# Probabilities copied in two parts, and the normalisations moved to ScalarE, in an attention kernel with a planned order

## The chip, the cores and the metric

The kernel runs on one core of one Trainium2 chip. The metric is the device time of one execution in microseconds (us). The core has five instruction streams: PE (TensorE, matrix products), DVE (VectorE), ACT (ScalarE), POOL (GpSimd) and SP (SyncE), which here only issues DMAs. Each stream works off its list in order; between streams, semaphores hold an instruction back until the other engine has passed a count. 16 DMA engines move data. A tile lies over 128 partitions; matrix products arrive in PSUM, which the kernel uses as 8 banks of 512 float32 columns.

## The reference

Input is x of shape (8, 512, 128): 8 batches, 512 positions, 128 features. With xn = layernorm(x) it computes

```
out = x + attention(xn) + ffn(xn)

attention:  q, k, v = xn @ W_qkv, 16 heads of 64; rotary embedding on q and k
            p = softmax(causal(q k^T / 8));   (p v) @ W_out
ffn:        q, k, v = xn @ Wq + bq, ...;      16 heads of 8, full softmax, no mask
            x2 = xn + layernorm(ctx @ Wo + bo)*g1 + be1
            gate = softmax(x2 @ Wg + bg); the two best of 8 experts, weighted
            x2 + layernorm(moe)*g2 + be2
```

All in float32. Three layer normalisations per batch: of x (called xn), of the inner attention's output (nm1) and of the experts' sum (nm2).

## The kernel before

The 8 batches are worked off one behind the other, each with T = 4 tiles of 128 positions. The causal attention of a batch goes in NC = 8 chunks c of two heads. For one chunk the steps are: `proj` (PE) makes q and k; `raw` (ACT) brings them to SBUF; `swap` (SP, L1134) exchanges neighbouring rows by two DMAs, for the rotary embedding; `rope`, `hi`, `lo` (POOL, L1196 to L1211) rotate and split them into two parts of reduced precision; `sc` (PE, L1694) makes the scores, in three units: unit 0 is query tile 3 with 512 keys, unit 1 is tiles 2 and 0 with 384 and 128, unit 2 is tile 1 with 256; `max` (DVE, L1580), `exp` (ACT, L1338); `tr` (DVE, L1588) transposes blocks of 32x32 of the probabilities in place, one step per unit; `shuf` (SP, L1140) copies them from `pn` to `pt` by four DMAs, one for each quarter of 32 source partitions, which completes the transposition; `pv` (PE, L1708) multiplies them with v; `div` (DVE, L1599) scales the result.

A tile of probabilities for 128 queries and 128 keys is "one tile" in `pn`; a chunk has 10 of them for each head (1 + 2 + 3 + 4). In `pn` and `pt` the 10 tiles of a head stand side by side, so a DMA moves runs of 2 heads x 10 tiles x 32 columns x 4 bytes = 2560 bytes, 128 runs in each. `pn` has two buffers, `pt` one: `shuf` also waits until `pv` of the chunk before is done.

The inner attention's steps (`fsm`, `fmax` L1458, `fmT`, `fst`, `fexp` L1293, `fpv` L1758 and others) stand between those of the chunks. The normalisations are done so: `ln`, `ln1`, `ln2` (DVE) make mean and variance and write `spread`; `rs0`, `rs1`, `rs2` (POOL, L1188) raise it to the power -0.5; `xn`, `nm1`, `nm2` (DVE, L1384) subtract the mean and multiply, in four instructions on 128x128. `x2` and `out` (POOL, L1218) work on with nm1 and nm2.

The order of each stream is written out by numbers: `PLACE` has a place for every step, and `ORDER` sorts the steps of an engine by it. `PSUM` has the bank of every product. `after(step)` is the semaphore and the count at which the step is done; `wait` leaves out what the stream has already waited for.

Of the kernel before, what the change touches and what calls it, by code (L numbers as in the profile page):

```python
# [9 lines left out]
ALU = mybir.AluOpType  # L10
ACT = mybir.ActivationFunctionType
# [3 lines left out]
P = 128  # L15
# [27 lines left out]
TILES_OF = {3: 0, 2: 4, 0: 7, 1: 8}  # L43
UNIT_TILES = [slice(0, 4), slice(4, 8), slice(8, 10)]
PT_N = T * (T + 1) // 2
# [13 lines left out]
        [78],  # L59
        [197],  # L60
        [326],
        [456],
        [585],
        [716],
        [842],
    ],
    "tt": [
        [5],
    ],
    "proj": [  # L70
# [8 lines left out]
    ],  # L79
    "tb": [  # L80
        [2],
    ],
    "fqk": [
        [1],
        [86],
        [213],
        [342],
        [472],
        [601],
        [729],  # L90
        [858],
    ],
    "fv": [
        [8],
        [121],
        [249],
        [378],
        [509],
        [636],
        [764],  # L100
        [897],
    ],
    "fsm": [
# [8 lines left out]
    ],  # L112
    "fmT": [
        [14, 30, 58, 83],
        [131, 153, 189, 212],
        [260, 282, 318, 343],
        [388, 411, 446, 471],
        [517, 540, 576, 600],
        [646, 668, 704, 730],
        [775, 798, 830, 857],  # L120
        [903, 926, 963, 985],
    ],
    "fst": [
# [8 lines left out]
    ],  # L132
    "fpv": [
# [8 lines left out]
    ],  # L142
    "sc": [
        [23, 26, 28, 35, 46, 47, 52, 53, 56, 73, 74, 75, 88, 93, 95, 101, 102, 104, 116, 119, 120, 124, 127, 129],
        [147, 148, 150, 161, 178, 179, 181, 182, 183, 203, 204, 205, 219, 220, 221, 228, 229, 237, 244, 247, 250, 254, 257,
         258],
        [276, 277, 279, 290, 307, 308, 310, 312, 314, 332, 333, 334, 348, 350, 351, 357, 358, 363, 375, 377, 379, 383, 384,
         387],
        [405, 406, 409, 419, 435, 437, 438, 441, 443, 461, 462, 463, 476, 480, 482, 485, 486, 492, 504, 505, 507, 512, 513,
         515],  # L150
        [534, 535, 536, 548, 564, 565, 567, 568, 571, 590, 591, 594, 605, 609, 611, 615, 616, 619, 633, 634, 637, 639, 644,
         645],
        [663, 664, 667, 677, 692, 693, 696, 697, 699, 719, 720, 721, 735, 736, 739, 744, 745, 753, 762, 765, 766, 770, 772,
         773],
        [792, 793, 796, 806, 822, 823, 825, 827, 831, 848, 849, 850, 862, 866, 868, 873, 874, 881, 891, 892, 895, 901, 902,
         904],
        [921, 922, 923, 935, 951, 952, 955, 957, 958, 976, 977, 978, 991, 993, 996, 1000, 1001, 1004, 1013, 1015, 1016, 1020,
# [3 lines left out]
        [31, 33, 38, 45],  # L161
        [154, 156, 160, 170],
        [283, 285, 289, 300],
        [412, 414, 418, 429],
        [542, 543, 547, 557],
        [670, 672, 676, 686],
        [799, 801, 805, 816],
        [928, 929, 934, 945],
    ],
# [9 lines left out]
    ],  # L179
    "fT": [  # L180
        [48, 71, 91, 114],
        [177, 199, 226, 243],
        [303, 330, 356, 373],
        [439, 457, 478, 499],
        [561, 587, 607, 631],
        [690, 714, 743, 758],
# [1663 lines left out]
```

## Time and profile before

| | us |
|---|---|
| median of three runs | 1407.32 |
| the three runs | 1400.66, 1407.32, 1414.51 |
| the profiled execution | 1420.66 |
| its span, first to last instruction | 1418.8 |

| engine | busy us | share of the span |
|---|---|---|
| PE | 1110.0 | 78% |
| DVE | 1034.0 | 73% |
| POOL | 857.6 | 60% |
| ACT | 742.4 | 52% |

The mean granted clock of TensorE is 0.861 of its full 2.4 GHz. The 16 DMA engines are busy 40% of the span by SP's queue and move 139 MB at 98 GB/s, 320 KB in each of the 256 DMAs of the probabilities. A share of busy time is a mean over stages; what stands in the way in one place is to be read from the chain of waits and the waits by engine.

### The profile page before, as it was taken

The numbers are of one execution on the slowest core, as the hardware profiler recorded it, in microseconds if no ns is written. First come the engines' busy times: TensorE is split into PE (matmuls) and PEld (weight loads), VectorE is DVE, ScalarE is ACT, GpSimd is POOL, SyncE is SP. The second block draws the span as 40 slices with busy tenths as digits, with TensorE's granted clock in tenths as the row PEclk, the third lists the DMA queues.
The fourth block names the chain that finished last, engine by engine and source line by source line (L and its number), as shares of the span: only waits on it lengthen the run. The fifth ranks groups of instructions, "written<-read, shape, count | busy, mean of one in ns | idle before, by whom it ended". The sixth has DMA issues, their size and how long they took to land.

```text
span 1418.8 us, 23791 instructions
## 1 busy us (share of the span) xinstructions
PE 1110.0 (78%) x8474; PEld 662.9 (47%) x8474; DVE 1034.0 (73%) x2404; ACT 742.4 (52%) x1665; POOL 857.6 (60%) x728
## 2 busy tenths in 40 slices
PE   4778789687886878887798777877889678897866
PEld 2334446344452444544464444544546335463534
DVE  6966679767786767965788657777768766787646
ACT  3656455564544645555455644547545464555731
POOL 3658766657665485576564756656676555744940
PEclk8799979899798978988889886998969888698978
DMA  5163632455224442434524363244542245425342
GB/s 158 41 135 86 147 88 60 108 127 119 64 73 110 116 121 60 96 87 116 123 64 108 83 147 77 68 104 112 124 108 71 72 96 119 112 64 123 81 93 66
DMA packets 77793, 139.27 MB, mean 98 GB/s; under 512 B 11494, under 2 KB 23016, under 8 KB 77676
## 3 DMA queue, kind: packets, MB, share of 16 engines
q1 hardware_dynamic: 74204, 134.80, 39.8%
q10 hardware_dynamic: 3472, 2.95, 0.7%
q8 instruction: 68, 1.11, 0.3%
q14 instruction: 49, 0.40, 0.1%
HBM read 5.60 MB, written 2.10 MB: 5 GB/s over the span
## 4 chain that ended last, share of the span: by engine, by line
PE 36%; DVE 20%; DMA 17%; SPq 12%; POOL 7%; issue 4%; ACT 3%; ACTq 1%; POOLq 0%; DVEq 0%
DMA pt<-pn 12%; PE work L1708 10%; SPq L1140 10%; DVE fnmax L1458 7%; PE work L1758 4%; PE work L1694 4%; DVE pn L1588 4%; DMA swapped<-raw 4%; PE work L1616 3%; PE work L1724 3%; PE work L1618 3%; PE work L1617 3%; PE work L1733 3%; DVE work L1540 2%; DVE branch L1543 2%
## 5 line engine op out<-in xcount | busy, mean ns | idle before, releaser
L1196 POOL TENSOR_TENSOR raw<-raw,cos_t 128x512 f32<-128x512 f32 x128 | 163.5, 1277 | 406.4 <-DMA swapped<-raw 390.5
L1293 ACT ACTIVATE fpt<-work 128x1024 f32<-128x1024 f32 x256 | 251.9, 1026 | 202.0 <-PE work L1748 192.7
L1458 DVE TENSOR_REDUCE fnmax<-work 128x2 f32<-128x1024 f32 x256 | 302.4, 1215 | 59.1 <-PE work L1733 58.0
L1338 ACT ACTIVATE pn<-work,nmax 128x512 f32<-128x512 f32 (+3 forms) x512 | 266.0, 537 | 140.5 <-DVE nmax L1580 139.8
L1708 PE MATMUL work<-pt,v 128*32 128x384 f32 (+2 forms) x2560 | 211.9, 493 | 118.0 <-DMA pt<-pn 113.1
L1580 DVE CUSTOM_DVE_ANT_0 work<-work,causal 128x512 f32<-128x512 f32 (+3 forms) x512 | 236.6, 515 | 81.2 <-PE work L1694 80.8
L1708 PEld LDWEIGHTS work<-pt,v 128*32 128x32 f32 x2560 | 100.2, 136 | 228.4 <-issue 154.7
L1588 DVE STREAM_TRANSPOSE pn<-pn 128x1024 f32<-128x1024 f32 (+1 forms) x192 | 198.6, 1048 | 3.3 <-ACT pn L1338 3.2
L1211 POOL TENSOR_TENSOR qk_l<-raw,qk_h 128x512 fp32r<-128x512 f32 x128 | 180.0, 1413 | 3.4
L1200 POOL TENSOR_TENSOR raw<-raw,swapped 128x512 f32<-128x512 f32 x128 | 164.3, 1284 | 10.0
L1197 POOL TENSOR_TENSOR swapped<-swapped,sin_t 128x512 f32<-128x512 f32 x128 | 164.6, 1286 | 0.0
L1599 DVE TENSOR_TENSOR u<-work,l_wide 128x512 f32<-128x512 f32 x64 | 43.8, 685 | 149.5 <-PE work L1708 140.7
L1318 ACT COPY raw<-work 128x512 f32<-128x512 f32 x128 | 75.3, 588 | 127.3 <-PE work L1618 84.9
L1758 PE MATMUL work<-fpt,fv 128*9 128x512 f32 x1024 | 140.5, 646 | 1.3 <-ACT pn L1338 1.3
L1694 PE MATMUL work<-qk_h 64*128 64x512 f32 (+3 forms) x512 | 105.2, 403 | 46.5 <-POOL qk_l L1211 23.3
L1733 PE MATMUL work<-fqs 32*128 32x512 f32 x512 | 73.8, 565 | 62.4 <-DVE fnmax L1458 18.4
L1206 POOL CAST qk_h<-raw 128x512 fp32r<-128x512 f32 x128 | 108.4, 859 | 14.6 <-PE work L1694 12.8
L1338 ACT ACTIVATION_READ_ACCUMULATOR pn<-work,nmax 128x1 f32 x512 | 108.5, 212 | 0.0
L1694 PEld LDWEIGHTS work<-qk_h 64*128 64x128 f32 x512 | 53.8, 201 | 105.0 <-issue 47.5
L1748 PE MATMUL work<-fqm,fqs 32*128 32x512 f32 x512 | 71.9, 549 | 32.2 <-DVE fnmax L1458 5.9
L1694 PE MATMUL work<-qk_l,qk_h 64*128 64x512 f32 (+3 forms) x512 | 90.5, 344 | 0.0
L1694 PE MATMUL work<-qk_h,qk_l 64*128 64x512 f32 (+3 forms) x512 | 90.2, 344 | 0.0
(153 smaller groups left out, 1893.0 us busy)
## 6 DMA issues: line engine op xcount, KB each, us to landing
pt<-pn SPq DMA_DIRECT2D x256, 320.0 KB, 5.7
swapped<-raw SPq DMA_DIRECT2D x256, 128.0 KB, 2.3
fqs<-fqn SPq DMA_DIRECT2D x96, 128.0 KB, 2.7
x_in<-in_L_attn_x_dram SPq DMA_DIRECT2D x8, 256.0 KB, 4.7
out_dram<-x_in SPq DMA_DIRECT2D x7, 256.0 KB, 2.3
fpt<-in_L_attn_W_qkv_dram ACTq DMA_DIRECT2D x3, 512.0 KB, 6.2
pn<-in_L_ffn_We_dram ACTq DMA_DIRECT2D x1, 512.0 KB, 9.7
wout<-in_L_attn_W_out_dram ACTq DMA_DIRECT2D x1, 512.0 KB, 12.5
```

Source lines behind the costliest of these rows:

```text
L1196: nc.gpsimd.tensor_tensor(raw[:, n % 3], raw[:, n % 3], cos_t[:], ALU.mult)
L1197: nc.gpsimd.tensor_tensor(swapped[:, n % 2], swapped[:, n % 2], sin_t[:], ALU.mult).then_inc(pool_link, 1)
L1200: nc.gpsimd.tensor_tensor(raw[:, n % 3], raw[:, n % 3], swapped[:, n % 2], ALU.add).then_inc(done["rope"], 1)
L1211: nc.gpsimd.tensor_tensor(turned(qk_l[:, c % 2, k], k), plain(raw[:, n % 3], k), turned(qk_h[:, c % 2, k].bitcast(F32), k), ALU.subtract). ...
L1293: nc.scalar.activation(fpt[:, ((b * G + g) * T + i) % FP, 2 * r:2 * r + 2].rearrange("p h n -> p (h n)"), bank_of(("fst", b, g, i), 2 * r, 2),
L1338: ins = nc.scalar.activation(pn[:, c % 2, :, h, tiles].rearrange("p c i r -> p i c r"), bank_of(("sc", b, c, unit), h)[:, at:at + n].rearr ...
L1458: nc.vector.tensor_reduce(fnmax[:, j, 2 * r:2 * r + 2, 0:1], bank_of(("fsm", b, g, j), 2 * r, 2).rearrange("p (f n) -> p f n", f=2), AX.X, ...
L1580: ins = nc.vector.tensor_tensor_reduce(out=scores, in0=scores, in1=causal[:, S - n:S], scale=-1.0 / math.sqrt(DH), scalar=3.0e38, op0=ALU.add,
L1588: nc.vector.transpose(blocks, blocks).then_inc(done["tr"], 1)
L1694: ins = nc.tensor.matmul(bank_of(x_, h)[:, at:at + (j + 1) * P], left[rows, c % 2, 0, tile(j)], right[rows, c % 2, 1, 0:(j + 1) * P], star ...
L1708: ins = nc.tensor.matmul(psum[a:a + STRIP, at:at + len(js) * P], v[:, i, 2 * c + h, a % DH:a % DH + STRIP], moving.rearrange("p a j r -> p ...
L1758: ins = nc.tensor.matmul(psum[f * STRIP:f * STRIP + FVW], fv[:, i, g * GH + f], fpt[:, ((b * G + g) * T + i) % FP, f], start=i == 0, stop= ...
```

## The change

1. `pn` and `pt` become two tiles each. Part 0 has the 8 tiles of units 0 and 1 (query tiles 3, 2 and 0), part 1 the 2 tiles of unit 2 (query tile 1). The step `shuf` copies part 0 in four DMAs with runs of 2048 bytes, 256 KB each, and waits for the transpose of unit 1; a new step `shu2` copies part 1 in four DMAs with runs of 512 bytes, 64 KB each, and waits for the transpose of unit 2. Both wait for `pv` of the chunk before; `pv` and the next use of `pn` wait for both. The four quarters are now issued in the order 0, 2, 1, 3.
2. `pv` has seven groups of four matmuls instead of five, since a product with three query tiles at once (384 columns) would reach over both parts; the number of columns is the same.
3. `xn`, `nm1`, `nm2` go from DVE to ACT, as an activation with scale and bias from columns: x * rstd + shift. DVE makes -mean in one more small instruction (L1413), POOL multiplies it with rstd in one more (L1201). DVE loses 96 instructions and gains 24, ACT gains 96, POOL gains 24.
4. Small single-column tiles are put together, and some loads at the start go to other places of SBUF, so that the tiles fit.
5. `PLACE` and `PSUM` are new throughout.

SP's list in the second batch, before, around the copies of its first three chunks (L1134 the swaps, L1140 the copies, L1147 copies for the inner attention):

```order
L1134 DMA swapped<-raw 64x512 x2
L1140 DMA pt<-pn 128x1x640 x4
L1134 DMA swapped<-raw 64x512 x6
L1140 DMA pt<-pn 128x1x640 x4
L1134 DMA swapped<-raw 64x512 x2
L1147 DMA fqs<-fqn 32x2x512
L1147 DMA fqs<-fqn 32x1024
L1147 DMA fqs<-fqn 32x2x512
L1134 DMA swapped<-raw 64x512 x2
L1140 DMA pt<-pn 128x1x640 x4
```

and the same three chunks after the change (L1144 the swaps, L1150 both copies: 128x1x512 is the large part, 128x1x128 the small one):

```order
L1150 DMA pt<-pn 128x1x128 x4
L1144 DMA swapped<-raw 64x512 x2
L1150 DMA pt<-pn 128x1x512 x4
L1144 DMA swapped<-raw 64x512 x4
L1150 DMA pt<-pn 128x1x512 x4
L1144 DMA swapped<-raw 64x512 x2
L1150 DMA pt<-pn 128x1x128 x4
L1157 DMA fqs<-fqn 32x2x512
L1157 DMA fqs<-fqn 32x1024
L1157 DMA fqs<-fqn 32x2x512
L1150 DMA pt<-pn 128x1x128 x4
L1144 DMA swapped<-raw 64x512 x2
```

The large copy of the third chunk follows as the next row. In the first and the third chunk the small part is issued ahead of the large one, in the second behind it. Over the whole program the small part stands first in 24 of 64 chunks.

DVE's list after the change, from the transpose of unit 1 of the second of these chunks to that of unit 2 (ISA rows are the masked maxima and the reads of their results):

```order
L1605 STREAM_TRANSPOSE pn<-pn 128x8x128
L1596 ISA work,nmax<-work,causal 128x256
L1596 ISA nmax 128x1
L1596 ISA work,nmax<-work,causal 128x512
L1596 ISA nmax 128x1
L1596 ISA work,nmax<-work,causal 128x512
L1596 ISA nmax 128x1
L1610 RECIPROCAL l_inv<-l_sum 128x8
L1596 ISA work,nmax<-work,causal 128x384
L1596 ISA nmax 128x1
L1596 ISA work,nmax<-work,causal 128x128
L1596 ISA nmax 128x1
```

The transpose of unit 2 is the next row. In the list before, two maxima and one `div` stood between the two transposes of this chunk; how much stands between them differs from chunk to chunk in both lists.

The diff, without the tables of numbers:

```diff
-TILES_OF = {3: 0, 2: 4, 0: 7, 1: 8}
-UNIT_TILES = [slice(0, 4), slice(4, 8), slice(8, 10)]
-PT_N = T * (T + 1) // 2
+PT_N = [2 * T, T // 2]
+PT_OF = {3: (0, 0), 2: (0, T), 0: (0, 2 * T - 1), 1: (1, 0)}
+UNIT_AT = [(0, slice(0, T)), (0, slice(T, 2 * T)), (1, slice(0, T // 2))]
...
     "xT": [
         [0],
-        [78],
-        [197],
+        [75],
+        [201],
...
-        pn = sb("pn", [P, 2, QUADS, 2, PT_N, STRIP])
-        pt = sb("pt", [P, QUADS, 2, PT_N, STRIP])
+        pn = [sb(f"pn{n}", [P, 2, QUADS, 2, tiles, STRIP]) for n, tiles in enumerate(PT_N)]
+        pt = [sb(f"pt{n}", [P, QUADS, 2, tiles, STRIP]) for n, tiles in enumerate(PT_N)]
...
-                elif kind == "shuf":
-                    c = x_[2]
-                    wait(sp, after("tr", b, c, 2))
+                elif kind in ("shuf", "shu2"):
+                    c, part = x_[2], int(kind == "shu2")
+                    wait(sp, after("tr", b, c, 1 + part))
                     wait(sp, after("pv", *ring(1, b, c, NC)))
-                    for a in range(QUADS):
-                        sp.dma_start(pt[:, a].rearrange("p h n r -> p (h n r)"),
-                                     pn[a * STRIP:(a + 1) * STRIP, c % 2].rearrange("p c h n r -> p c (h n r)")).then_inc(shuf_done[c % 2], 16)
+                    for a in (0, 2, 1, 3):
+                        sp.dma_start(pt[part][:, a].rearrange("p h n r -> p (h n r)"),
+                                     pn[part][a * STRIP:(a + 1) * STRIP, c % 2].rearrange("p c h n r -> p c (h n r)"))                            .then_inc((shuf_done, shu2_done)[part][c % 2], 16)
...
-                    nc.gpsimd.tensor_tensor(rstd[:, n], spread[:, n], power[:], ALU.pow).then_inc(done[kind], 1)
+                    nc.gpsimd.tensor_tensor(rstd[:, n], spread[:, n], power[:], ALU.pow).then_inc(pool_link, 1)
+                    links += 1
+                    pool.wait_ge(pool_link, links)
+                    nc.gpsimd.tensor_tensor(shift[:, n], shift[:, n], rstd[:, n], ALU.mult).then_inc(done[kind], 1)
...
+            def normalise(kind, n, dst, src):
+                for t in range(T):
+                    ins = nc.scalar.activation(dst(t), src(t), ACT.Identity, scale=rstd[:, n, t:t + 1], bias=shift[:, n, t:t + 1])
+                ins.then_inc(done[kind], 1)
...
+                elif kind == "xn":
+                    wait(act, after("rs0", b))
+                    wait(act, after("x2T", b - 2))
+                    wait(act, after("res", b - 2))
+                    normalise("xn", 0, lambda t: xn[:, b % 2, t], lambda t: x_in[:, b % XB, t])
...
+                nc.vector.tensor_scalar(shift[:, n].unsqueeze(2), moments[:, n, :, 0:1], -1.0, None, ALU.mult)
                 nc.vector.tensor_scalar(spread[:, n].unsqueeze(2), moments[:, n, :, 1:2], EPS, None, ALU.add)\
                     .then_inc(done[kind], 1)
-
-            def normalise(kind, n, dst, src):
-                for t in range(T):
-                    ins = nc.vector.tensor_scalar(dst(t), src(t), moments[:, n, t, 0:1], rstd[:, n, t:t + 1],
-                                                  ALU.subtract, ALU.mult)
-                ins.then_inc(done[kind], 1)
...
                     wait(pe, landed("shuf", b, c))
+                    wait(pe, landed("shu2", b, c))
                     if c == 0:
                         wait(pe, after("vc", b, T - 1))
-                    for i, js in ((0, (3, 2, 1)), (0, (0,)), (1, (3, 2, 1)), (2, (3, 2)), (3, (3,))):
-                        first, at = TILES_OF[js[0]] + i, (T - 1 - js[0]) * P
+                    for i, js in ((0, (3, 2)), (0, (0,)), (0, (1,)), (1, (3, 2)), (1, (1,)), (2, (3, 2)), (3, (3,))):
+                        part, first = PT_OF[js[0]]
+                        first, at = first + i, (T - 1 - js[0]) * P
```

## Rows read from the trace of the kernel before

**Rows 1.** The page, part 1: busy us of each engine (share), instructions.

```profile
PE 1110.0 (78%) x8474; PEld 662.9 (47%) x8474; DVE 1034.0 (73%) x2404; ACT 742.4 (52%) x1665; POOL 857.6 (60%) x728
```

**Rows 2.** The page, part 4: the chain that ended last, by engine and line.

```profile
PE 36%; DVE 20%; DMA 17%; SPq 12%; POOL 7%; issue 4%; ACT 3%; ACTq 1%; POOLq 0%; DVEq 0%
DMA pt<-pn 12%; PE work L1708 10%; SPq L1140 10%; DVE fnmax L1458 7%; PE work L1758 4%; PE work L1694 4%; DVE pn L1588 4%; DMA swapped<-raw 4%; PE work L1616 3%; PE work L1724 3%; PE work L1618 3%; PE work L1617 3%; PE work L1733 3%; DVE work L1540 2%; DVE branch L1543 2%
```

**Rows 3.** Chain in order of time, one chunk: start us, us, what.

```profile
889.55 0.59 SPq L1140
...
890.83 1.98 SPq L1140
...
892.85 5.98 DMA pt<-pn
...
898.97 2.37 PE work L1708 x40
```

**Rows 4.** Chain in order of time, the PV step of another chunk.

```profile
775.16 4.50 PE work L1708 x40
```

**Rows 5.** Windows, both PV steps: us, PE, PEld, DVE, ACT, POOL busy; PEclk, DMA, GB/s.

```profile
775.10:779.70 4.60, 4.54 (x44) 2.16 (x44) 0.00 (x0) 0.00 (x0) 0.01 (x1) 0.50 0.33 101
898.90:901.40 2.50, 2.43 (x42) 1.48 (x44) 0.48 (x1) 1.00 (x5) 2.42 (x3) 1.00 0.57 180
```

**Rows 6.** Chain in order of time, a swap behind a copy.

```profile
104.97 4.16 DMA swapped<-raw
```

**Rows 7.** Waits: of PV before L1708; of POOL: us, times, longest.

```profile
  DMA pt<-pn: 147.2, 50
...
POOL raw L1196 <- DMA swapped<-raw: 390.5, 75, 15.3
```

**Rows 8.** The page, part 6: DMA issues, KB each, median us to landing.

```profile
swapped<-raw SPq DMA_DIRECT2D x256, 128.0 KB, 2.3
...
out_dram<-x_in SPq DMA_DIRECT2D x2, 128.0 KB, 1.8
```

**Rows 9.** Timeline of SP's queue at the start: start us, us, line.

```profile
10.97 0.43 SPq L1124 DMA_DIRECT2D affine<-in_L_ffn_be_dram  x1
```

**Rows 10.** Windows as in rows 5, through one copy with nothing beside it.

```profile
196.00:197.25 1.25, 1.25 (x9) 1.25 (x7) 1.25 (x2) 0.59 (x1) 0.00 (x0) 0.50 0.91 104
197.25:198.50 1.25, 1.25 (x8) 1.25 (x7) 0.13 (x1) 0.00 (x0) 0.00 (x0) 0.50 1.02 221
198.50:199.75 1.25, 1.25 (x8) 0.93 (x7) 0.39 (x2) 0.00 (x0) 0.00 (x0) 0.50 0.88 131
199.75:201.00 1.25, 1.25 (x12) 0.13 (x8) 1.05 (x9) 0.89 (x1) 0.04 (x1) 0.50 0.87 268
```

**Rows 11.** Groups by form, DVE: busy us, mean ns, idle before.

```profile
L1384 DVE TENSOR_SCALAR branch<-branch,moments,rstd 128x128 f32<-128x128 f32 x32 | 20.1, 699 | 1.7 <-POOL rstd L1188 1.7
...
L1384 DVE TENSOR_SCALAR xn<-x_in,moments,rstd 128x128 f32<-128x128 f32 x32 | 14.9, 532 | 0.0
...
L1384 DVE TENSOR_SCALAR branch<-work,moments,rstd 128x128 f32<-128x128 f32 x32 | 10.9, 402 | 7.7 <-POOL rstd L1188 7.7
...
L1379 DVE TENSOR_SCALAR spread<-moments 128x4 f32<-128x4 f32 x24 | 7.0, 291 | 0.8
```

**Rows 12.** Chain in order of time, the longest piece of L1384.

```profile
1122.36 4.93 DVE branch L1384 x4
```

**Rows 13.** Groups by form, PE, ACT, POOL: busy us, mean ns, idle before.

```profile
L1708 PE MATMUL work<-pt,v 128*32 128x384 f32 x1024 | 150.4, 664 | 118.0 <-DMA pt<-pn 113.1 <-ACT pn L1338 4.9
...
L1708 PE MATMUL work<-pt,v 128*32 128x128 f32 x1024 | 66.0, 331 | 0.0
...
L1708 PE MATMUL work<-pt,v 128*32 128x256 f32 x512 | 51.7, 475 | 0.0
...
L1338 ACT ACTIVATE pn<-work,nmax 128x128 f32<-128x128 f32 x128 | 48.3, 377 | 0.0
...
L1188 POOL TENSOR_TENSOR rstd<-spread,power 128x4 f32<-128x4 f32 x24 | 24.4, 1019 | 84.2 <-DVE spread L1379 84.2
```

More of the change, by code:

```diff
@@ L91 @@
-        [858],
+        [338],
+        [471],
+        [600],
+        [730],
+        [859],
     ],
     "fv": [
[L94 to L101, printed above, removed]
+        [6],
+        [115],
+        [242],
+        [377],
+        [505],
+        [633],
+        [760],
+        [890],
     ],
     "fsm": [
[8 rows of a table removed]
[8 rows of a table added]
     ],
     "fmT": [
-        [14, 30, 58, 83],
-        [131, 153, 189, 212],
-        [260, 282, 318, 343],
@@ L260 @@
     "smh": [
-        [2],
+        [5],
     ],
     "wh": [
-        [0, 1, 10],
+        [0, 2, 4],
+    ],
+    "xn": [
+        [1],
+        [52],
+        [169],
+        [309],
+        [437],
+        [557],
+        [688],
+        [823],
     ],
@@ L403 @@
-        [994],
+        [138],
+        [267],
+        [397],
+        [525],
+        [654],
+        [783],
+        [912],
+        [1015],
+    ],
+    "nm1": [
+        [145],
+        [274],
+        [403],
+        [533],
+        [661],
+        [790],
+        [922],
+        [1024],
     ],
     "x2h": [
-        [151],
-        [278],
-        [403],
-        [531],
-        [656],
-        [781],
-        [908],
-        [1005],
+        [155],
+        [284],
+        [413],
+        [542],
+        [671],
+        [800],
+        [929],
+        [1030],
@@ L414 @@
     ],
     "gexp": [
-        [156],
-        [283],
-        [409],
-        [535],
-        [661],
-        [787],
-        [913],
-        [1011],
+        [160],
+        [293],
+        [418],
+        [547],
+        [676],
+        [805],
+        [934],
+        [1034],
+    ],
+    "nm2": [
+        [198],
+        [338],
+        [468],
+        [579],
+        [715],
+        [856],
+        [968],
+        [1037],
     ],
@@ L427 @@
         [12],
-        [98],
-        [264],
-        [391],
-        [542],
-        [704],
-        [847],
+        [95],
+        [261],
+        [401],
+        [547],
+        [678],
+        [830],
     ],
     "turn": [
-        [8],
-    ],
-    "str": [
-        [4],
-    ],
-    "xn": [
-        [2],
-        [40],
-        [216],
-        [364],
-        [509],
-        [650],
-        [801],
-        [945],
-    ],
-    "strl": [
-        [5],
-    ],
-    "wl": [
-        [1, 7, 21],
-    ],
-    "xl": [
-        [6],
-        [91],
-        [227],
-        [375],
-        [526],
-        [669],
-        [812],
-        [959],
-    ],
-    "sml": [
-        [3],
-    ],
+        [4],
+    ],
+    "str": [
+        [2],
+    ],
+    "strl": [
+        [3],
+    ],
+    "wl": [
+        [1, 6, 7],
+    ],
+    "xl": [
+        [5],
+        [88],
+        [228],
+        [372],
+        [515],
+        [652],
+        [796],
+        [943],
+    ],
+    "sml": [
+        [8],
+    ],
     "qkb": [
-        [9],
+        [10],
     ],
@@ L608 @@
+        [298],
+        [441],
+        [583],
+        [727],
+        [869],
+        [1011],
+        [1121],
     ],
     "ln1": [
-        [163],
-        [308],
-        [455],
-        [601],
-        [746],
+        [159],
+        [303],
+        [446],
+        [590],
+        [733],
+        [876],
+        [1020],
+        [1126],
+    ],
+    "x2l": [
+        [173],
+        [316],
+        [459],
+        [602],
+        [745],
+        [888],
+        [1030],
+        [1140],
+    ],
@@ L615 @@
+    "gsub": [
+        [177],
+        [320],
+        [463],
+        [607],
+        [750],
         [893],
-        [1040],
-        [1149],
-    ],
-    "nm1": [
-        [166],
-        [312],
-        [458],
-        [604],
-        [750],
-        [896],
-        [1041],
+        [1035],
+        [1143],
+    ],
+    "pick": [
+        [179],
+        [327],
+        [464],
+        [608],
+        [751],
+        [894],
+        [1036],
+        [1145],
+    ],
+    "moew": [
+        [186, 190, 191, 192],
+        [329, 333, 334, 335],
+        [472, 476, 477, 478],
+        [615, 619, 620, 621],
+        [758, 762, 763, 764],
+        [901, 905, 906, 907],
+        [1043, 1047, 1048, 1049],
+        [1147, 1148, 1149, 1151],
+    ],
@@ L979, in build @@
         power = sb("power", [P, T])
-        spare = sb("spare", [P, 1])
-        value_bias = sb("value_bias", [P, 1])
-        warm = sb("warm", [P, 1])
+        singles = sb("singles", [P, 3])
+        spare, value_bias, warm = (singles[:, n:n + 1] for n in range(3))
         x_in = sb("x_in", [P, XB, T, D])
@@ L1015, in build @@
         spread = sb("spread", [P, 3, T])
+        shift = sb("shift", [P, 3, T])
         rstd = sb("rstd", [P, 3, T])
-        gmax = sb("gmax", [P, T])
-        gsum = sb("gsum", [P, T])
-        grec = sb("grec", [P, T])
+        gate_cols = sb("gate_cols", [P, 3, T])
+        gmax, gsum, grec = (gate_cols[:, n] for n in range(3))
         gexp = sb("gexp", [P, T, E])
@@ L1043, in build @@
         shuf_done = [sem(f"shuf{n}_done") for n in range(2)]
+        shu2_done = [sem(f"shu2{n}_done") for n in range(2)]
         x_loaded = [sem(f"x{n}_loaded") for n in range(XB)]
@@ L1288, in _ @@
                     if b == 0:
+                        wait(act, after("tt", 0))
                         for n in range(3):
@@ L1484, in _ @@
                     statistics("ln1", 1, lambda t: src[:, t])
-                elif kind == "nm1":
-                    src = bank_of(("wo", b)).rearrange("p (t d) -> p t d", d=D)
-                    wait(dve, after("rs1", b))
-                    wait(dve, after("out", b - 1))
-                    normalise("nm1", 1, lambda t: branch[:, t], lambda t: src[:, t])
                 elif kind == "gsub":
```

600 lines of the change are left out of this document (268 added, 332 removed), and 441 rows, old and new, of tables (PLACE, PSUM).

## The prediction

> **What bounds the kernel now.** I read the page's busy shares first [rows 1]: the busiest engine, PE, works 78% of the span. No engine is full, so the time lies in waits between engines that each take their work in a fixed order. The chain that ended last says which waits [rows 2]: PE 36%, DVE 20%, DMA 17%, SP's queue 12%. By line, the copy pt<-pn (12%), its issues (L1140, 10%) and the PV matmuls behind it (L1708, 10%) are a third of the chain. One chunk in order of time shows the link [rows 3]: SP starts its four issues right behind the last transpose, at 889.55; the third takes 1.98 us where the first takes 0.59; the last byte lands at 898.83, 9.3 us after the first issue; then PV runs. The waits agree [rows 7]: PE and its weight loader stand 147 us for this copy, 50 times, 2.9 us each.
>
> Two things hang on that copy. After such a wait PE is slow: the same 40 PV instructions take 2.37 us in one chunk [rows 3] and 4.50 us in another [rows 4], with a granted clock of 1.00 and 0.50 [rows 5], that is 2.4 and 1.2 GHz; before the slow ones PE had stood idle for the copy. And the swap DMAs of the rotary embedding wait in SP's queue behind the copy: at 104.97 the chain goes through one that needs 4.16 us to land [rows 6], where 2.3 is the median [rows 8]. Swaps are 4% of the chain, some 50 us, so 12 pieces of this size; pt<-pn, 12.4% of 1418.8 us at 6.0 us each, is 28 or 29 pieces. About 40 of 64 chunks have their copy on the chain in one way or the other.
>
> **The change, term by term**, in us against the profiled execution's own 1420.66 (span 1418.8).
>
> *A, early start of the large part.* The copy of the tiles of units 0 and 1 no longer waits for the last transpose. What this gives depends on the new order. In it 24 of the 64 chunks have the small copy ahead of the large one in SP's queue, as the first and third chunk shown there; there SP waits for the last transpose before anything moves, and nothing starts early. In 18 of the other 40 the two transposes stand next to each other on DVE (under 1 us of work between). In 22 there is DVE work between, 1.2 to 11 us by the durations of its rows; the piece shown for DVE is some 3.6 us. Where it is long, the path from the last transpose shrinks from 9.3 us to four issues at about 0.6 and a landing like that of 128 KB in 512-byte runs, 1.8 us [rows 8]: 4.4 us, so at most 4.9 is gained. Cut off at that, the 22 gain 3.2 on average, 70 us together; 24 of these fall to chunks 0 and 7 of a batch, which have 10 us and more of other PE work before PV. The other 46, at a chance of about a half of being on the chain: **-22**. Bounds 0 and -45.
>
> *B, swaps behind the copy.* Eight issues stand before a swap instead of four. Four issues of 128 runs cost 0.43 us each when the queue is free [rows 9], 0.6 in the copy itself: 1.7 to 2.4 us later, less what the large ones gain by moving 256 KB instead of 320. 12 pieces at +0.8: **+10**. Bounds 0 and 12 x 2.4 = +29.
>
> *C, chunks without a gap.* The same bytes in eight DMAs. The large ones start 0.6 us earlier, the added issues and completions eat that. 42 chunks, of which 18 on the chain, at +0.3: **+5**. Bounds -0.6 and +1.2 each: -11 and +22.
>
> *D, order of the four quarters (0, 2, 1, 3).* The diff also changes this. In a copy with nothing beside it the rate falls to 131 GB/s in one stretch of 1.25 us and is 268 in the next [rows 10]; with 130 + 276 KB before it, the slow stretch lies in the second quarter of 328 KB and the fast one mostly in the third. If the slow one ran like the fast one, a set would save 0.64 us, 40 sets 26. I take half: **-13**. Bounds +12 (the mixture disturbs, 0.3 a set) and -52 (twice the gain). The Trainium skill (SBUF — State Buffer, section Door 1: The DMA port swizzle) says that partitions 0 to 63 reach only the 8 even DMA ports and 64 to 127 the odd ones, which would make quarters 0 and 1 rivals and 0 and 2 not. The same section also says that the ports are picked by one transfer's span and two transfers can't be fused; by that this term would be nothing and the sum 13 higher.
>
> *E, DVE.* The normalisations go: 20.1 + 14.9 + 10.9 = 45.9 us; 24 copies of the mean are added at 0.29 us, 7.0 [rows 11]. Of the 39 us saved little is on the path: L1384 is under the 2% at which the chain's list ends, with one long piece of 4.93 us in which DVE went at a quarter of its pace beside POOL [rows 12]. **-7**, bounds 0 and -20 (all at DVE's share, 20 of 73%, is 11).
>
> *F, ScalarE.* 96 new instructions on 128x128. Nearest row: the exponential of the same shape, with one column operand, 377 ns [rows 13]; 36 us. ScalarE is 3% of the chain at 52% busy, so a sixteenth: **+2**, bounds 0 and +15 (normalisations held up in its queue). The Trainium skill (ScalarE: Activation LUTs, section What ACT_TABLE_LOAD costs) gives 186 ns + 0.833 ns per element and 93 ns for each column operand; with two that is an estimate of 479 ns, 46 us, and would change this term by less than one. The same page's rules for kernel authors send such adds and multiplies to VectorE; no row shows the rule deciding here, where ScalarE is the freer engine.
>
> *G, POOL.* 24 more tiny operations at 1.02 us [rows 13], 24 us, on the way to every normalised tile; POOL's share of the chain is a ninth of its busy time: **+3**, bounds 0 and +15.
>
> *H, PV.* Seven groups of four matmuls instead of five, the same columns. Busy per group: 384 columns 150.4/256 = 0.59 us, 256 columns 51.7/128 = 0.40, 128 columns 66.0/256 = 0.26 [rows 13]. Before 2 x 0.59 + 0.40 + 2 x 0.26 = 2.10; now 3 x 0.40 + 4 x 0.26 = 2.24. With 44 PV steps on the chain (10.4%, 148 us, so 3.4 us each), a part of them at half clock: **+8**, bounds +6 and +18.
>
> *I, clock.* PV is 1.0 us a chunk above its fast 2.37. If five of the shortened waits leave PE warm, at 2.1 each: **-10**, bounds +5 and -25.
>
> Sum: -22 + 10 + 5 - 13 - 7 + 2 + 3 + 8 - 10 = **-24 us**, 1.7%. The profiled execution is 13 us above the median of the three runs (1407.32); 1.7% of that is 24 as well, so **1384 us** is the forecast, 1397 for a profiled execution like this one. The order on PE I count at nothing: between one PV and the next it has the same kinds of steps in nearly the same places in both.
>
> **Rivals.**
>
> *R1, slower: SP's queue becomes the wait.* Third and fourth issues of a set take 1.9 us [rows 3], because the queue accepts no more until something ahead of it is done. If that is counted in DMAs or runs and not in bytes, the added four do not cost 0.6 but more. Place: the chunks without a gap and the swaps, 18 + 12 on the chain. It decides from about 0.8 us an issue on, where it has eaten the 24; at 1.0 us it is 4 x 0.4 x 30 = +48, so +24: **1431**. For it: the 1.98; and POOL already stands 390 us for swaps [rows 7]. Against it: small issues in a row at 0.43 [rows 9]. The Trainium skill (DMA: Bandwidth & Descriptors, section Bandwidth) tells to batch DMAs to 1 MiB and gives about 2.0 us + bytes/436e3 for each; paid one after the other for four more DMAs of 64 KB that would be an estimate of 8.6 us a chunk. The trace does not bear this out for a set: four of 320 KB would be 11 us by it, and land in 9.3.
>
> *R2, no change: the waits only move.* The new order uses the early start in 22 chunks alone; DVE's maxima and PE's own work take over as the chain (20 and 36% already), D is worth nothing. Then -24 + 13 + 11 = 0: **1407**.
>
> *R3, more: the copy itself gets faster.* If quarters from both halves run as the fast stretch does, -1.3 us a set, and the waits fall under what cools PE: D -52, I -20, the rest as it is: -24 - 39 - 10 = -73: **1335**. For it: the rate halves where nothing else moves. Against: the first stretch is slow too, and no order changes that.
>
> **How the numbers follow.** Forecast 0.38, R2 0.27, R3 0.18, R1 0.17. What can be told from no change is 1%, 14 us. Faster than 1393: R3, most of the forecast (0.32) and a little of R2 (0.04): 0.54. Within: 0.27. Slower than 1421: R1 and a little of R2: 0.19. The range from 1342 to 1424 cuts off about half of R3 and half of R1, one in ten on each side; the bounds of A and D, not added up, lie within it. The forecast's own range is 1365 to 1400.
>
> **What would show it.** A: first large issue ahead of the last transpose in about 22 chunks; PE's wait for pt down from 147 to 110 us or so; if it stays, A is wrong. B and R1: the issue durations of the 512-byte copies, 0.6 or near 1.9; POOL's wait for swaps beyond 390. D: first issue to last landing of the large part under 7.4 us (four fifths of 9.3). E, F: DVE busy near 995, ScalarE near 780. H: L1727 busier by about 9 us at the same clock. I: mean granted clock over 0.87. What would make it wrong above all is D, which no row measures, and an order that is worse on DVE in a way that counts of rows do not show.

## The result: 2% slower, and the profile after

| | before | after |
|---|---|---|
| median of four runs each, us | 1406.02 | 1434.65 |
| lowest and highest | 1400.66, 1414.51 | 1432.18, 1442.0 |
| the profiled execution, us | 1420.66 | 1432.18 |
| mean granted clock in it | 0.861 | 0.853 |

The ratio is 1.0207 with an interval of 1.0143 to 1.027: the change made the kernel slower by 29 us. The forecast was 1384 us, 24 us faster, with a range from 1342 to 1424.

Busy us of each engine after, as in [rows 1], and the chain that ended last, as in [rows 2]:

```profile
PE 1103.1 (77%) x9498; PEld 697.0 (49%) x9498; DVE 993.1 (69%) x2332; ACT 776.3 (54%) x1761; POOL 862.2 (60%) x752
...
PE 43%; DVE 20%; SPq 14%; DMA 8%; ACT 7%; issue 6%; POOL 3%; ACTq 0%; DVEq 0%; POOLq 0%
```

DVE lost 41 us of work and ScalarE gained 34, as foreseen. The chain has less DMA (8% for 17%) and more PE (43% for 36%). So the transfers hold up the end less. The waits of the engines (us in total, times, longest), and the one for the copy in the kernel before:

```profile
POOL raw L1209 <- DMA swapped<-raw: 377.6, 70, 16.8
DVE u L1616 <- PE work L1727: 207.2, 41, 9.1
PEld work L1727 <- issue: 198.7, 224, 8.2
...
PE work L1727 <- DMA pt<-pn: 140.3, 33, 8.0
```

```profile
PE work L1708 <- DMA pt<-pn: 113.1, 38, 5.3
```

PE's wait for the copy went from 113 us in 38 pieces to 140 in 33, and the longest from 5.3 us to 8.0: fewer waits, and longer ones. The issues (KB each, median us to landing), first before and then after, rule out that DMAs got slower:

```profile
pt<-pn SPq DMA_DIRECT2D x256, 320.0 KB, 5.7
...
pt<-pn SPq DMA_DIRECT2D x256, 256.0 KB, 4.4
swapped<-raw SPq DMA_DIRECT2D x256, 128.0 KB, 2.1
pt<-pn SPq DMA_DIRECT2D x256, 64.0 KB, 2.2
```

A swap took 2.3 us before [rows 8]. A long wait is then to be looked for ahead of the issue. In the third chunk of the third batch, SP's queue, then DVE, then PE (start us, us, engine, line):

```profile
436.91 6.46 SPq L1144 DMA_DIRECT2D swapped<-raw  x4
443.47 6.83 SPq L1150 DMA_DIRECT2D pt<-pn  x8
```

```profile
433.57 1.23 DVE L1605 STREAM_TRANSPOSE pn<-pn 128x1024 f32<-128x1024 f32 x1
...
439.74 0.70 DVE L1605 STREAM_TRANSPOSE pn<-pn 128x512 f32<-128x512 f32 x1
```

```profile
454.25 4.50 PE L1727 MATMUL work<-pt,v 128*32 128x256 f32 x56 [6.58 <-DMA pt<-pn]
```

The transpose of unit 1 ends at 434.80. From there on the large copy could go: the PV of the chunk before is done. But SP's list has four issues of swaps first; these wait for ScalarE's `raw`, the third of them until 442.3, and end at 443.4. Then comes the small copy, 3.5 us, and only then the large one, at 447.0: **12.2 us after its inputs were ready**, and 6.6 after the last transpose. PE stands for 6.58 us, and its clock is at half after that:

```profile
451.00:454.20 3.20, 0.00 (x0) 0.00 (x0) 0.00 (x0) 0.91 (x3) 1.59 (x2) 0.50 0.61 170
454.20:458.80 4.60, 4.55 (x60) 3.01 (x60) 0.00 (x0) 0.00 (x0) 0.00 (x0) 0.50 0.00 0
```

(Windows as in [rows 5]; the granted clock is the 0.50.) Over all 64 chunks, I took for each copy (after the change, for each large one) the moment at which its last transpose and the PV before it had ended, and its first issue. Before, the issues lay 27 us behind these moments in all. After, the large ones lay 247 us behind: by the step that stands directly ahead, 16 chunks behind a swap that itself waited (113 us), 16 behind their own small copy (112; in the chunk above the swaps stood ahead of that in turn), the rest behind copies for the inner attention and a load. By the position of the chunk in its batch, the third is the worst: its first large issue came 0.7 us after the last transpose before, and 8.8 after the change. That is the theory for the experiments.

### The profile page after: what moved, and what is told of

It reads as the page before. It is cut to its first block, busy times and chain, and to the rows that moved or that the text cites. A ratio compares the mean times of both kernels' runs of the same rounds, so it can differ in the third digit from the quotient of the medians.

```text
span 1430.3 us, 26155 instructions
## 1 busy us (share of the span) xinstructions
PE 1103.1 (77%) x9498; PEld 697.0 (49%) x9498; DVE 993.1 (69%) x2332; ACT 776.3 (54%) x1761; POOL 862.2 (60%) x752
## 3 DMA queue, kind: packets, MB, share of 16 engines
q8 instruction: 76, 1.25, 0.4%
## 4 chain that ended last, share of the span: by engine, by line
PE 43%; DVE 20%; SPq 14%; DMA 8%; ACT 7%; issue 6%; POOL 3%; ACTq 0%; DVEq 0%; POOLq 0%
PE work L1727 12%; SPq L1150 11%; DVE fnmax L1482 7%; DMA pt<-pn 6%; PE work L1633 5%; PE work L1635 4%; PE work L1634 4%; PE work L1711 4%; DVE pn L1605 3%; DVE work L1596 3%; PE work L1777 3%; PE work L1752 3%; ACT pn L1372 2%; ACT fpt L1313 2%; PE work L1767 2%
## 5 line engine op out<-in xcount | busy, mean ns | idle before, releaser
L1209 POOL TENSOR_TENSOR raw<-raw,cos_t 128x512 f32<-128x512 f32 x128 | 163.6, 1278 | 377.9 <-DMA swapped<-raw 377.6
L1727 PE MATMUL work<-pt,v 128*32 128x128 f32 (+1 forms) x3584 | 212.7, 406 | 168.3 <-DMA pt<-pn 140.3
L1727 PEld LDWEIGHTS work<-pt,v 128*32 128x32 f32 x3584 | 142.8, 139 | 240.8 <-issue 198.7
L1777 PE MATMUL work<-fpt,fv 128*9 128x512 f32 x1024 | 137.5, 635 | 0.7 <-ACT pn L1372 0.7
L1711 PE MATMUL work<-qk_h 64*128 64x512 f32 (+3 forms) x512 | 101.9, 391 | 24.0 <-POOL qk_l L1224 6.4
L1711 PEld LDWEIGHTS work<-qk_h 64*128 64x128 f32 x512 | 50.9, 193 | 80.4 <-issue 28.2
L1711 PE MATMUL work<-qk_l,qk_h 64*128 64x512 f32 (+3 forms) x512 | 86.4, 330 | 0.0
L1711 PE MATMUL work<-qk_h,qk_l 64*128 64x512 f32 (+3 forms) x512 | 86.3, 329 | 0.0
```

The source lines that it names most:

```text
L1209: nc.gpsimd.tensor_tensor(raw[:, n % 3], raw[:, n % 3], cos_t[:], ALU.mult)
L1711: ins = nc.tensor.matmul(bank_of(x_, h)[:, at:at + (j + 1) * P], left[rows, c % 2, 0, tile(j)], right[rows, c % 2, 1, 0:(j + 1) * P], star ...
L1727: ins = nc.tensor.matmul(psum[a:a + STRIP, at:at + len(js) * P], v[:, i, 2 * c + h, a % DH:a % DH + STRIP], moving.rearrange("p a j r -> p ...
L1777: ins = nc.tensor.matmul(psum[f * STRIP:f * STRIP + FVW], fv[:, i, g * GH + f], fpt[:, ((b * G + g) * T + i) % FP, f], start=i == 0, stop= ...
```

## The experiments

The intervals are of the ratio to the kernel before, run beside it on the same chip (medians 1414.79, 1415.92 and 1413.21 us for the three groups of experiments, 1406.02 for the change itself). A comparison of two rows is therefore one of ratios. "PE idle before PV" is all idle time there, whatever ended it. "Late" is the sum just described; "slow PV" counts PV steps over 3.2 us of 64. In the kernel before PE had stood idle 3.2 us on average ahead of the slow ones, and 0.3 us ahead of the others.

| kernel | median us | ratio | interval | PE idle before PV, us | late, us | slow PV |
|---|---|---|---|---|---|---|
| before | 1414 | 1 | | 118 | 27 | 35 |
| the change | 1434.65 | 1.021 | 1.014–1.027 | 168 | 247 | 35 |
| large copies early | 1362.04 | 0.964 | 0.958–0.970 | 97 | 9 | 25 |
| pairs turned | 1394.29 | 0.985 | 0.980–0.990 | 125 | 103 | 25 |
| new plan, one copy | 1495.53 | 1.057 | 1.051–1.063 | 217 | 123 | 39 |
| quarters alone | 1373.67 | 0.971 | 0.965–0.976 | 84 | 26 | 26 |
| quarters 0, 3, 1, 2 | 1373.07 | 0.971 | 0.967–0.975 | 85 | 27 | 22 |
| quarters 1, 0, 3, 2 | 1405.17 | 0.994 | 0.991–0.997 | 100 | 27 | 28 |
| normalisations alone | 1431.66 | 1.012 | 1.007–1.017 | 112 | 26 | 31 |
| old plan, split | 1341.46 | 0.945 | 0.941–0.950 | 57 | 114 | 18 |
| the same, quarters in order | 1348.21 | 0.955 | 0.949–0.961 | 62 | 115 | 16 |
| the same, normalisations on ScalarE | 1355.15 | 0.958 | 0.953–0.964 | 49 | 119 | 13 |
| old plan, split, copies early | 1339.11 | 0.944 | 0.938–0.949 | 41 | 12 | 13 |
| large copies early, normalisations on DVE | 1393.53 | 0.987 | 0.983–0.991 | 97 | 8 | 25 |

### 1. The large copies moved forward in SP's list

All else is the changed kernel, with 32 such moves:

```diff
+BEFORE_ON_SP = [(('shuf', 0, 0), ('swap', 0, 2, 1)), ..., (('shuf', 2, 2), ('swap', 2, 4, 1)), ...]
+for step, other in BEFORE_ON_SP:
+    ORDER["SP"].remove(step)
+    ORDER["SP"].insert(ORDER["SP"].index(other) if other else len(ORDER["SP"]), step)
```

> The changed kernel, with 32 of its 64 large copies moved forward in SP's list to the place where, by the changed kernel's trace, their inputs are ready; nothing else. Theory 1 (SP's new list issues the large copies late: 246 us of lateness over the program, against 27 before): the lateness goes, PE's wait for pt falls from 168 us to under 120, and the time falls from 1435 to 1375-1400, below before. Theory 2 (the split costs: eight issues, seven groups of matmuls): it stays at 1425 or above. Theory 3 (the normalisations on ScalarE, or the new order on PE, DVE and ACT, cost): it falls a little but stays above 1415.

Measured 0.964, 1362 us, more than the first theory expected: from 2% slower than before to 3.6% faster, 5.6% of the time by moving no instruction but these on SP. The same chunk, SP and PE:

```profile
424.34 3.30 SPq L1155 DMA_DIRECT2D pt<-pn  x4
427.74 5.36 SPq L1149 DMA_DIRECT2D swapped<-raw  x4
433.14 2.54 SPq L1155 DMA_DIRECT2D pt<-pn  x4
```

```profile
437.35 2.38 PE L1732 MATMUL work<-pt,v 128*32 128x256 f32 x56
```

The large copy goes at once, 5.6 us ahead of the end of the last transpose (429.96). PV starts 7.4 us after that transpose instead of 13.8, without a wait, and at the full clock. The swaps that now stand behind it did not suffer (POOL waited 377.6 us for them after the change):

```profile
POOL raw L1214 <- DMA swapped<-raw: 322.5, 64, 17.3
...
PE work L1732 <- DMA pt<-pn: 96.6, 32, 6.5
```

Half of the cure, the small copy put behind the large one in the 24 chunks where it stood ahead:

```diff
+BEFORE_ON_SP = [... each of 24 large copies in front of its own small one ...]
```

> The changed kernel, with only the 24 pairs turned round in which the small copy stood ahead of the large one. Theory 1: part of the gain of the larger move, since the rest of the lateness stands behind swaps: 1400-1425. Theory 2 and 3: 1430 or more.

Measured 0.985, 1394 us, a little under the expected 1400 to 1425: 3.5% of the 5.6. The late issues fall to 103 us, 75 of them behind swaps. Both kinds of lateness cost.

### 2. The new plan without the split

```diff
-PT_N = [2 * T, T // 2]
+PT_N = [T * (T + 1) // 2]
...
-                    for i, js in ((0, (3, 2)), (0, (0,)), (0, (1,)), (1, (3, 2)), (1, (1,)), (2, (3, 2)), (3, (3,))):
+                    for i, js in ((0, (3, 2, 1)), (0, (0,)), (1, (3, 2, 1)), (2, (3, 2)), (3, (3,))):
```

One copy of 320 KB at the later of the two places; orders, quarters and normalisations as in the change.

> The changed kernel without the split: one tile again, four copies of 320 KB in the order 0, 2, 1, 3, at the later of the two places in SP's list; the new order of all engines and the normalisations on ScalarE stay. Compared with the quarters alone on the old order (0.9705 of before) it tells what the new lists cost without the split. If it is SP's places of the copy, behind swaps: 1410-1435, some 3-4% above the quarters alone. If the new lists are harmless without the split: 0.965-0.98.

Measured 1.057, beyond both expectations: nearly 9% above the same copy on the old plan (0.971, experiment 3, with the normalisations still on DVE, which by themselves cost 1.2%). The plan lets PE stand 217 us before PV, 84 there. Most of these 133 us can be read from the two traces. The new SP list issues this copy late too, 123 us in all for 26, mostly behind swaps. And PE has less other work between the last transpose and PV, 531 us over the 64 chunks for 575. So the plan needs the early copy; the change as it is gives it that copy in 31 of 64 chunks, experiment 1 in 56. On this plan the split as it stands in the change is worth 3.6% of the time before (1.057 to 1.021), and 9.3% with the copies moved as in experiment 1.

### 3. Parts of the change on the old plan

The order of the quarters alone:

```diff
-                    for a in range(QUADS):
+                    for a in (0, 2, 1, 3):
```

> The kernel before, with one line changed: the four quarters of a copy are issued in the order 0, 2, 1, 3. If the issue order of the quarters is what makes the copies of the changed kernel faster (the four large issues take 3.3 us in all there, 5.1 before), four issues fall from 5.1 to about 3.9 us, the copy lands 1 to 2 us earlier, and the time falls by 15 to 45 us, to 1360-1390. If it is the smaller size of each DMA instead, nothing changes: 1400-1412.

Measured 0.971. The four issues take 4.3 us instead of 5.1, the landing 5.0 instead of 5.7, and from the first issue to the last landing it is 8.6 us instead of 9.5 (medians). The rate in eight stretches of 1.25 us from the first issue on, in the first copy of the second batch (windows; the last column is GB/s; six of the eight):

```profile
209.95:211.20 1.25, 1.25 (x9) 1.01 (x6) 0.84 (x5) 0.80 (x2) 0.00 (x0) 1.00 0.96 98
211.20:212.45 1.25, 1.25 (x8) 0.75 (x8) 1.13 (x16) 1.25 (x3) 0.00 (x0) 1.00 0.88 166
212.45:213.70 1.25, 0.82 (x6) 0.34 (x6) 1.15 (x7) 1.25 (x2) 0.00 (x0) 1.00 0.86 289
213.70:214.95 1.25, 0.96 (x8) 0.74 (x9) 0.86 (x3) 0.91 (x3) 0.00 (x0) 1.00 0.96 209
214.95:216.20 1.25, 1.25 (x13) 1.25 (x12) 1.25 (x2) 0.02 (x1) 0.00 (x0) 1.00 0.91 324
216.20:217.45 1.25, 1.25 (x14) 1.25 (x13) 1.25 (x3) 0.00 (x0) 0.00 (x0) 1.00 0.51 183
```

Is it this order, or that neighbours in time come from different halves of the partitions? Two more orders:

```diff
-                    for a in range(QUADS):
+                    for a in (0, 3, 1, 2):
```

> The kernel before, its four quarters issued in the order 0, 3, 1, 2. Theory (what helps is that quarters next to each other in time are of different halves of the partitions, 0 to 63 and 64 to 127): as with 0, 2, 1, 3, so 0.970 of before, first issue to last landing 7 to 8 us and not 9.3. Rival (it is the order 0, 2, 1, 3 itself, which ends on the quarter that PV needs last, or chance in the queue): 0.99 to 1.00.

```diff
-                    for a in range(QUADS):
+                    for a in (1, 0, 3, 2):
```

> The control: the kernel before with the quarters in the order 1, 0, 3, 2. Another order, but neighbours in time are of the same half of the partitions, as in 0, 1, 2, 3. Theory of the halves: no change, 0.997 to 1.003, and rates in a copy as before. Rival (any order other than the rising one helps, or which quarter is last matters): 0.97 to 0.985.

Measured 0.971 and 0.994. The other order that alternates between the halves gives all of it; the one that does not gives 0.6%, where nothing was expected and the interval leaves 0.3 to 0.9%, for which I have no reason. In the kernel with 1, 0, 3, 2 the same copy goes as in the kernel before (there 106, 215, 158, 285, 193, 219 and 89 GB/s from the second stretch to the eighth), with its slow fourth stretch, and is still moving in the eighth:

```profile
215.60:216.85 1.25, 1.25 (x7) 0.78 (x7) 1.13 (x16) 1.25 (x3) 0.00 (x0) 1.00 1.02 225
216.85:218.10 1.25, 0.75 (x6) 0.27 (x4) 1.15 (x7) 1.25 (x2) 0.00 (x0) 1.00 0.88 143
218.10:219.35 1.25, 1.02 (x9) 0.80 (x10) 0.85 (x3) 0.87 (x3) 0.00 (x0) 1.00 0.88 283
219.35:220.60 1.25, 1.25 (x14) 1.25 (x13) 1.25 (x2) 0.00 (x0) 0.00 (x0) 1.00 0.89 181
220.60:221.85 1.25, 1.25 (x13) 1.25 (x13) 1.25 (x3) 0.00 (x0) 0.00 (x0) 1.00 0.77 229
221.85:223.10 1.25, 1.25 (x10) 1.17 (x10) 0.52 (x3) 0.78 (x2) 0.00 (x0) 1.00 0.29 97
```

The split with all that belongs to it, on the old order of every engine, the small copy right behind its large one, normalisations on DVE:

```diff
+PLACE["shu2"] = [[at + 0.5 for at in row] for row in PLACE["shuf"]]
```

> The order of before on every engine, normalisations on DVE as before, with the copy in two parts (the small one right behind the large one in SP's list), quarters 0, 2, 1, 3, and PV in seven groups. Theory 1: the split and the quarters are a gain when SP issues the large part at its old place: 1365-1395. Theory 2 (the split costs): 1415-1435.

Measured 0.945, 1341 us, better than the 1365 to 1395 expected, the best but one of all, and 7.4% below the change (0.945 over 1.021). The large copy starts ahead of the last transpose in 48 of 64 chunks here. PE's wait for the copy and POOL's for the swaps:

```profile
POOL raw L1199 <- DMA swapped<-raw: 311.5, 70, 13.7
...
PE work L1717 <- DMA pt<-pn: 50.8, 26, 4.2
```

With the quarters in their old order:

```diff
-                    for a in (0, 2, 1, 3):
+                    for a in range(QUADS):
```

> As the split on the order of before, but with the quarters in the old order 0, 1, 2, 3. If the two gains are separate (quarters -2.9%, whole -5.5%), the split alone is worth 2.6%: 0.974 of before, 1370-1385, with four large issues back at about 4.1 us. If eight issues only pay with the faster quarters, 1395-1415.

Measured 0.955, where 0.974 was expected. So the split is worth 4.5% by itself, the quarters 3% by themselves, and both together 5.5%: they shorten the same wait.

The normalisations alone, on the old plan, at the moments at which DVE did them:

```diff
+for step, other in BEFORE_ON_ACT:
+    ORDER["ACT"].remove(step)
+    ORDER["ACT"].insert(ORDER["ACT"].index(other) if other else len(ORDER["ACT"]), step)
```

> The kernel before, with the three normalisations on ScalarE (scale and bias from columns) at the places in ScalarE's list where they ran on DVE by the trace. By the terms of the prediction (DVE -7, ScalarE +2, POOL +3) nothing that can be measured: ratio 0.99-1.01. Theory 3 (they cost): 1.01-1.02.

Measured 1.012, and on top of the split:

```diff
+BEFORE_ON_ACT = [... the same 24 steps ...]
```

> The split and the quarters on the order of before (0.9454), and the normalisations on ScalarE as well. If they are worth nothing measurable: 0.94-0.95. If DVE's relief pays once the copy is short: 0.93-0.94. If they cost: 0.955.

Measured 0.958 (0.957 without the longest of its five runs), so 1.2 to 1.4% above 0.945.

This kernel has every part of the change; only the orders of the engines are the old ones. So the new plan is what separates it from the change: 1.021 over 0.958 is 6.5%. The 32 moves on SP in experiment 1 bring the new plan to 0.964, within the intervals of 0.958 (0.958 to 0.970, and 0.953 to 0.964). What the new plan cost was the places of the large copies in SP's list, and hardly anything else that the time shows.

In the kernel with the normalisations alone DVE is busy 994 us instead of 1034, and waits more:

```profile
POOL raw L1204 <- DMA swapped<-raw: 409.3, 75, 16.9
...
DVE u L1607 <- PE work L1716: 156.3, 40, 8.0
...
DVE work L1588 <- PE work L1702: 103.6, 65, 5.3
...
DVE fnmax L1474 <- PE work L1741: 66.7, 57, 5.0
```

Before, the last three were 140.7, 80.8 and 58.0 us: 47 us more waiting for 40 of work saved. What made PE later was not taken apart; ScalarE, on which the scores depend through `raw`, has 35 us more in its queue, and POOL's wait for swaps is 19 us longer.

### 4. What is left

On the old plan with the split, 16 large copies still stood behind steps that waited. Moved forward in the way of experiment 1:

```diff
+BEFORE_ON_SP = [(('shuf', 0, 0), ('swap', 0, 3, 0)), (('shuf', 0, 1), ('swap', 0, 3, 1)), ..., (('shuf', 7, 2), ('fdup', 7, 3))]
```

> The kernel before with the split, the new quarter order and DVE's normalisations kept (b_split), and 16 large copies moved forward in SP's list, each in front of the first step that was issued after the copy's inputs were ready (15 swaps and one copy for the inner attention stood ahead). In b_split the first issues of these 16 lay 0.8 to 15 us behind that moment, 101 us together. Theory (the place of the large copy in SP's list is what counts): five of them are first chunks of a batch with 10 us of other PE work before PV and give nothing; the others, about 40 us, show by a third to a half: 0.005 to 0.015 below b_split's 0.945 of before, so 0.930 to 0.940. POOL's wait for swaps may grow by some us. Rival (b_split has little wait left to save, PE stood 57 us before PV in all): the same as b_split within 0.003, or slower by up to 0.005 because each swap now stands behind its copy.

Measured 0.944, the same as 0.945 within the intervals; 0.930 to 0.940 was expected: the rival was right. PE's idle time before PV fell by 16 us,

```profile
PE work L1722 <- DMA pt<-pn: 33.8, 16, 3.8
```

but the time hardly moved. By its chain PE and DVE hold 62% of the end, where it was 56% in the kernel before [rows 2] and 60% with the split before these moves; DMA holds 6%, where it was 17% and 6%:

```profile
PE 37%; DVE 25%; SPq 13%; POOL 8%; DMA 6%; issue 5%; ACT 5%; ACTq 0%; POOLq 0%; DVEq 0%
```

And the changed kernel with early copies, its normalisations given back to DVE:

```diff
+for step, other in BEFORE_ON_DVE:
+    ORDER["DVE"].remove(step)
+    ORDER["DVE"].insert(ORDER["DVE"].index(other) if other else len(ORDER["DVE"]), step)
```

> The changed kernel with its 32 late large copies moved forward (a_sp) and the three normalisations back on DVE, each in front of the transpose or maximum that ran next when ScalarE did it. Theory (the loss of the change is the late copies, and the normalisations on ScalarE cost 1.2% by themselves): a_sp was 0.964 of before, so 0.950 to 0.955, and 0.005 to 0.01 above b_split at 0.945. Rival (the new plan of the other engines was made for normalisations on ScalarE and suffers when DVE gets 46 us back): 0.960 to 0.970. Second rival (the rest of the new plan is worse than the old by more than the normalisations): the same as a_sp, and then the gap to b_split belongs to the orders of PE, DVE and ACT.

Measured 0.987, 2.4% worse than with ScalarE, against my theory and outside both rivals' ranges. PE waits for the copy as before (93.6 us), but the path to the normalised tile is longer:

```profile
POOL branch L1238 <- DVE branch L1407: 42.3, 13, 11.1
```

against 26.2 us when ScalarE did it. By themselves these 16 us do not make up the difference of 32 us. The sign of this move depends on the plan around it. I chose the places on DVE by the times in a trace, so part of the 2.4% may be those places; that stays open.

## Why the prediction was wrong

**The step that failed is A**, and in it two sentences: that in 24 chunks with the small copy ahead "nothing starts early", and the bounds "0 and -45". No early start was the best case there, not the only one. An issue in SP's list waits for everything ahead of it: the small copy for the last transpose, the swap for ScalarE. (By the Trainium skill, DMA: Bandwidth & Descriptors, section Anatomy of one DMA — SWDGE (gpsimd) path, waits for semaphores happen on the issuing sequencer and not in the DMA engines; the timeline of the queue agrees, with a large copy 12.2 us late while its data lay ready.) I counted how many copies could start early and never asked when the steps ahead of each copy become ready. The lists shown with the change have it: in the third chunk of the second batch the small copy and two swap issues stand ahead of the large one, and in the chunk of the third batch shown above four swap issues and the small copy. The term should have had a positive bound; with 32 chunks late by 247 us in all and 80 us lost to it (experiment 1 against the change), it was the largest of all, and it was left out. It is more than the 51 us between the forecast and the measured time. "The order on PE I count at nothing" was the smaller part of it: the kinds of steps are the same, but PE has 531 us of other work between the transposes and PV where it had 575 (experiment 2). The term that was missing is the order on SP.

- The early start itself was undersized. On the old plan, where it happens in 48 chunks, the split with the old order of the quarters gave -4.5%, 64 us, for the -9 us to which A, B, C, H and I add up on the new one. With it went slow PV steps (16 for 35) and POOL's wait for swaps (318 us for 390). How the 64 us divide among these was not measured.
- B (+10) and C (+5): the cost of the issues is there, its consequence is not. With the quarters in their old order, eight issues take 7.3 us a chunk (4.2 and 3.1) where four took 5.1, within B's 1.7 to 2.4 us more; in the change, with the faster quarters, they take 6.4 (3.4 and 3.0). But the swaps behind go out faster: an issue of a swap while a copy is in flight took 1.3 us on average before, and 0.6 with the split alone. POOL waited 378 us for swaps after the change, 390 before. **R1's mechanism** did not decide: the small issues took 0.7 us on average, below the 0.8 from which it was to decide, and POOL's wait did not go beyond 390. Its number, 1431, was nearly the result, for another reason: luck. The Trainium skill (DMA: Bandwidth & Descriptors, section Anatomy of one DMA — SWDGE (gpsimd) path) gives a fixed part of about 2 us for each DMA, for DMAs that GpSimd issues; paid one after the other, four more would be an estimate of 8 us a chunk. The traces do not agree: the split alone added 2.2 us of issue time a chunk, and the kernel was 64 us faster.
- D (-13, bounds +12 and -52) had the right mechanism and a third of its size: -41 us alone, **R3's mechanism**. A set was to save 0.64 us and saved about 1, in all 64 chunks. The Trainium skill (SBUF — State Buffer, section Door 1: The DMA port swizzle) ties partitions 0 to 63 and 64 to 127 to different ports, and all three orders agree with that. That the ports are the reason no run shows. The page's sentence that two transfers cannot be fused (section "Can I just issue two DMAs to hit both halves?") did not keep the alternation from helping.
- E, F and G: the durations were right (DVE 993 us busy for 995 foreseen, ScalarE 776 for 780). The effect was not: the three terms sum to -2, the move alone measured +17. The rules for kernel authors of the Trainium skill (ScalarE: Activation LUTs), by which such work belongs on VectorE, agree with the old plan, and not with the last experiment.
- H (+8) did not show: a PV step at the full clock takes 2.38 us in seven groups, 2.37 in five [rows 3], and L1727 is busy 212.7 us against 211.9. Half-clock ones take 4.50 in both [rows 4].
- I (-10) had the wrong sign. As many PV steps were slow as before (35), and the granted clock fell from 0.861 to 0.853. Where the waits did get short, fewer PV steps were slow (25 and 18) and the mean granted clock went up: 0.874 with early copies, 0.882 with the split on the old plan.
- R2 (1407) did not come either. What it names, DVE and PE as the chain, is what ends the gains at 0.944.

Of the signs named beforehand, large issues ahead of the last transpose came in 31 chunks, above the 22; the large part took 7.3 us from first issue to last landing, under D's 7.4, but with 256 KB an issue (320 KB in the same order: 8.6); PE's wait, with its weight loader, went from 147 to 150 and not to 110, which by the prediction's own words says that A is wrong. The prediction named an order that is worse on DVE as a danger; the danger was on SP.

## What to carry to other kernels

When a planned order moves DMAs, walk the issuing queue's list and write beside each entry when its inputs are ready: a DMA goes out at the latest of all the times ahead of it, so one entry that waits holds up everything behind it. Take lateness (first issue minus inputs ready) from the trace for each copy; here it found 247 us in one table where busy shares and DMA sizes showed an improvement. A split of a transfer is worth trying on the old order first: it needed no new plan to give 4.5%, and 5.5% together with the order of the quarters. And when a change has two parts that touch one number, compare that number with each part alone: SP's issue time, 639 us before and 638 after, looked as if eight issues were free.

## What the hardware showed that I had not expected

- Four DMAs from quarters of 32 partitions are faster when neighbours in time come from different halves (0 to 63, 64 to 127): 3% of the kernel, and 4.3 us for four issues instead of 5.1. Another order that stays within the halves leaves it at 5.1.
- How long the third and fourth issues take depends on that too. The four issues last 0.58, 0.64, 1.92 and 1.86 us in the old order, 0.58, 0.61, 2.20 and 0.78 in the new, 0.58, 0.63, 2.19 and 0.83 with 0, 3, 1, 2, and 0.58, 0.64, 1.87 and 1.85 with 1, 0, 3, 2.
- Eight DMAs for the bytes of four cost SP issue time, but less than twice: with the quarters in their old order the copies take 449 us of issues over the whole kernel for 320, and the swaps 146 for 226, so 678 in all for 639; with 0, 2, 1, 3 it is 653 for 565. In a set of four, the third and fourth issues last 1.92 and 1.86 us with 320 KB each, 1.16 and 1.64 with 256 KB (1.27 and 0.71 in the order of the change). What they wait for no run shows.
- A `nm2` instruction of the kernel before (DVE, subtract and multiply, 128x128) lasts 0.33 to 0.34 us where POOL stands idle, and up to 1.64 us beside a busy POOL. On ScalarE the same work takes 0.47 to 0.51 us on average.
